# Running the ffn of a selective-scan block for two rows at a time, and summing softplus on TensorE

## The chip, the cores and the metric

One core of one Trainium2 chip. The metric is the time on the device in microseconds of one execution of the whole program; a kernel's figure is the median of several runs.

## What is computed

The input x is an image batch of 8 x 48 x 48 tokens with 256 channels, all float32. The block is:

```python
x = x + ss2d(ln(x))                      # L0_conv
t = x.reshape(8, 48 * 48, 256)
t = t + ffn(ln(t))                       # L0_ffn
```

`ss2d` projects to 512 channels twice (xh and z), runs a depthwise 3 x 3 convolution on xh, derives from it dt (rank 8, then `softplus`), B and C (16 states each), and scans over all 2304 positions:

```python
dtN = softplus(dt) @ W_dtN + b_dtN
h = exp(softplus(dt) * A) * h + (dtN * B) * x_t        # 512 channels x 16 states, 8 images
y = sum_n(h * C) + Dskip * x_t
out = (layernorm(y) * silu(z)) @ W_out + b_out
```

`ffn` is no matrix product. It reads three 16-wide one-hot fields and three flags of each normalised token (the first element over 0.5 of each field), shifts an 8-bit number by a 4-bit amount to the left or to the right, and adds 2.0 at the places of the low and of the high nibble of the result, in channels 64 to 87:

```python
hot = x > 0.5
val = first16(32) + 16 * first16(40); sa = first16(48)
res = where(act_shl, (val << sa) & 255, where(act_shr, val >> sa, 0))
out = x; out[64:80] += amp * one_hot(res & 15); out[72:88] += amp * one_hot(res >> 4)
```

Since t + ffn(ln(t)) holds t twice, once plain and once normalised, the kernel has to scale and shift each token's 256 channels once more: res * (1 + rs2) - mean * rs2.

## The kernel before

**Steps and rows.** The scan has 2304 steps, one for each position; a row of the image is 48 steps (slots 0 to 47), and four steps are a quad. The 128 partitions of the state hold 2 halves of the channels x 8 images x 8 pairs of states; each step works on 256 channels x 2 states in the free dimension. VectorE owns the first 192 of the 256 channels, GpSimd the other 64.

For each step VectorE runs four instructions: `decay_state` (L894 and L897: decay times the last state, one for each of the two states) and `add_input` (L910 and L913: x times db, plus that). The decays come from ScalarE: `decay` (L668) fills a PSUM tensor `ps_a` for two steps, with two such buffers, so ScalarE can be at most some two to three steps ahead of VectorE; `decay_pool` (L678) does the same for GpSimd, four steps at a time. GpSimd runs `pool_input` (L1161, the product of x and db for a quad), `pool_decay` (L1171) and `pool_add` (L1181). TensorE sums the states with C (`sum_states`, L510) after each quad, over a ring of 8 steps, and adds the skip term.

**Side work.** Everything else of a row, before and after its scan, is laid between the steps of other rows. The table `AT` (L40) says for each stage the step at which each of its parts is due, counted from the row's first step: `"ffn": (96, 96, 97, ...)` means that the ffn of row r runs while row r + 2 is scanned, its first two parts in slot 0. Each engine walks through all rows and slots in program order and does what is due. On VectorE `between(i, s, place)` is called twice per step: place 0 lies between `decay_state` and `add_input`, place 1 behind `add_input`; ffn parts with an even number go to place 0, those with an odd one to place 1. On ScalarE and GpSimd the side work stands behind the step's own instructions. All engines are in order, so a wait in a side part holds the decays or states behind it. Two PSUM banks (`ps_s`) are shared by all of TensorE's stages in turn.

**The softplus chain.** For row r, in slots relative to its first step: the convolution (-48 to -44) is copied to `xc`, projected (-43) and gives dt before softplus in the shared banks (-42 and -39). ScalarE's `softplus_parts` (L718 and L719) writes |dt| to `dt` and relu(dt) to `dttok`; `softplus_exp` and `softplus_log` (L725 and L730, both at -35, that is slot 13) make log(1 + exp(-|dt|)) of `dt` in place. GpSimd's `finish_dt` (L1201, at -34 and -29) adds the two. Then TensorE transposes the sum (L588, -26 to -23) and projects it to dtN (L597, -21); ScalarE's `copy_dttok` (L707) brings the tokens to `dttok`, which by then is free, and SP's queue stores them to DRAM (L377), from where they are loaded back, spread over the partitions, as `dtb` (L402). x goes the same way: `transpose_xc` (L565), `copy_xtok` (L703) to `xtok`, twelve stores for a row (L368), loads to `xb` (L393).

**The ffn.** After the output projection VectorE adds the residual (L973), takes statistics (L978, L984), ScalarE makes the reciprocal deviation (L770, L774), and VectorE runs `ffn_stage` 0 to 11, `ffn_mark`, `ffn_weigh`, `ffn_add_low` and `ffn_add_high` (L995 to L1053) on 3 blocks of 128 tokens: stage 0 has three L995 (the normalised first 64 channels), stage 1 the three scalings of the whole residual L1001, the others work on a few elements per partition, such as L1013, L1018 and L1029 with 3. Each stage waits by semaphore for the one before. SP's queue then stores the row (L436, slot 7) and loads the next residual (L431).

## Time and profile before

| | us |
|---|---|
| median of 3 runs | 3854.43 |
| lowest and highest | 3844.46, 3861.37 |
| the profiled execution | 3850.34 |
| its span | 3848.5 |
| busy in it: VectorE | 3545.4 (92%) |
| GpSimd | 3123.7 (81%) |
| TensorE matmul | 3007.7 (78%) |
| ScalarE | 2946.9 (77%) |
| mean granted TensorE clock | 0.858 |
| DMA | 790.44 MB, mean 205 GB/s |

The profile calls the engines PE (TensorE matmul), PEld (its weight loads), DVE (VectorE), ACT (ScalarE), POOL (GpSimd) and SPq (the queue that issues the DMAs). L12 is line 12 of the kernel. A group of instructions shows its count, busy time and mean; consecutive instructions of one engine overlap by some tens of nanoseconds, so that the distance from start to start says what one costs when the engine is full. The idle time of an engine is put down to what ended it. A windows line gives the stretch and its length in us, then the busy time in it (and the count of instructions) of PE, PEld, DVE, ACT and POOL, then the granted TensorE clock as a share of full speed, the busy share of the DMA engines and the GB/s that they moved.

### The profile page before, as it was taken

How to read it: one execution, taken by the hardware profiler on the slowest of the kernel's cores; microseconds unless marked ns; L12 is line 12 of the kernel's file. 1: busy time of each engine (PE TensorE's matmuls, PEld its weight loads, DVE VectorE, ACT ScalarE, POOL GpSimd, SP SyncE). 2: the span in 40 equal slices, each digit the busy share in tenths (PEclk: the TensorE clock that was granted, in tenths of full speed). 3: DMA queues.
4: the chain of work that ended last, by engine and by line, in shares of the span. 5: the costliest groups of instructions: out<-in, count | busy, mean ns of one | idle time of the engine just before them, and what ended most of it. 6: DMA issues, size and time to landing. Idle time of an engine off the chain costs nothing.

```text
span 3848.5 us, 105654 instructions
## 1 busy us (share of the span) xinstructions
PE 3007.7 (78%) x34944; PEld 1624.3 (42%) x34944; DVE 3545.4 (92%) x12174; ACT 2946.9 (77%) x6050; POOL 3123.7 (81%) x5772
## 2 busy tenths in 40 slices
PE   4787888788778887888788878877887788778765
PEld 2344444444444444444444444444444444444332
DVE  2699999999999999999999999999999999999997
ACT  2678777887787778787888787778887888787764
POOL 0688888888888888888888888888888888888885
PEclk7788888888888998888799888988888889988877
DMA  2878887887788878887888778778887888788874
GB/s 60 214 196 216 223 212 201 215 226 205 206 214 220 210 209 211 216 215 209 210 223 215 207 209 223 207 205 208 221 218 205 214 212 222 205 213 217 211 189 105
DMA packets 397438, 790.44 MB, mean 205 GB/s; under 512 B 94553, under 2 KB 249178, under 8 KB 396890
## 3 DMA queue, kind: packets, MB, share of 16 engines
q1 hardware_dynamic: 396890, 783.68, 78.4%
q8 instruction: 277, 4.54, 0.5%
q14 instruction: 271, 2.22, 0.2%
HBM read 648.20 MB, written 96.73 MB: 194 GB/s over the span
## 4 chain that ended last, share of the span: by engine, by line
DVE 43%; ACT 22%; PE 17%; issue 8%; DMA 3%; POOL 3%; SPq 2%; ACTq 0%; POOLq 0%; DVEq 0%
DVE h L910 9%; DVE ps_a L894 7%; ACT ps_a L668 7%; DVE ps_a L897 6%; DVE h L913 6%; PE ps_s L615 4%; PE ps_y L510 3%; ACT ap L678 3%; PE ps_s L577 3%; DVE sz L966 2%; DVE res L1001 2%; ACT y L753 2%; ACT yn L803 2%; PE ps_y L494 2%; ACT xtok L703 2%
## 5 line engine op out<-in xcount | busy, mean ns | idle before, releaser
L668 ACT ACTIVATE ps_a<-dtb,a_n 128x384 f32<-128x384 f32 x2304 | 1252.8, 580 | 387.5 <-DVE h L913 375.7
L1181 POOL TENSOR_TENSOR h<-mp,up 128x128 f32<-128x128 f32 x2304 | 1056.6, 459 | 392.3 <-PE ps_y L510 171.1
L1171 POOL TENSOR_TENSOR mp<-ap,h 128x128 f32<-128x128 f32 x2304 | 1053.9, 457 | 111.3 <-ACT ap L678 0.8
L894 DVE TENSOR_TENSOR ps_a<-ps_a,h 128x192 f32<-128x192 f32 x2304 | 817.4, 355 | 162.1 <-ACT ps_a L668 158.6
L910 DVE SCALAR_TENSOR_TENSOR h<-xb,db,ps_a 128x192 f32<-128x192 f32 x2304 | 923.5, 401 | 7.3 <-PE ps_y L510 4.2
L913 DVE SCALAR_TENSOR_TENSOR h<-xb,db,ps_a 128x192 f32<-128x192 f32 x2304 | 929.7, 404 | 0.0
L510 PE MATMUL ps_y<-h,cw 64*32 64x256 f32 x18432 | 771.3, 453 | 126.1 <-POOL h L1181 75.8
L897 DVE TENSOR_TENSOR ps_a<-ps_a,h 128x192 f32<-128x192 f32 x2304 | 810.0, 352 | 0.0
L678 ACT ACTIVATE ap<-dtb,a_n 128x256 f32<-128x256 f32 x1152 | 521.6, 504 | 154.1 <-POOL h L1181 127.8
L1161 POOL TENSOR_TENSOR up<-xb,db 128x512 f32<-128x512 f32 x576 | 611.5, 1062 | 0.0
L510 PEld LDWEIGHTS ps_y<-h,cw 64*32 64x32 f32 x18432 | 317.1, 120 | 490.4 <-issue 244.0
L546 PE MATMUL ps_s<-xs,conv_w 96*32 96x384 f32 x4608 | 399.3, 496 | 4.9 <-ACT xc L686 4.9
L529 PE MATMUL ps_s<-xlnT,win 128*128 128x384 f32 x768 | 277.9, 507 | 53.4 <-ACT xlnT L780 53.4
L536 PE MATMUL ps_s<-xlnT,win 128*128 128x384 f32 x768 | 289.2, 509 | 14.8 <-DVE sz L966 13.1
L565 PE MATMUL ps_s<-ident,xc 128*128 128x128 f32 x576 | 137.3, 396 | 207.9 <-ACT xtok L703 194.1
L615 PE MATMUL ps_s<-wout,yn 128*128 128x256 f32 x1152 | 288.9, 394 | 2.4 <-POOL yn L1206 2.4
L577 PE MATMUL ps_s<-xp,wdt 9*128 9x192 f32 x768 | 206.0, 675 | 104.9 <-ACT xp L695 99.5
L1201 POOL TENSOR_TENSOR dt<-dt,dttok 128x768 f32<-128x768 f32 x96 | 174.1, 1814 | 91.9 <-ACT dt L730 91.9
L615 PEld LDWEIGHTS ps_s<-wout,yn 128*128 128x128 f32 x1152 | 208.1, 190 | 80.4 <-issue 50.4
L546 PEld LDWEIGHTS ps_s<-xs,conv_w 96*32 96x32 f32 x4608 | 141.5, 111 | 237.5 <-issue 231.5
L607 PE MATMUL ps_s<-swap,y 128*128 128x128 f32 x576 | 141.2, 393 | 122.6 <-ACT y L753 101.7
L494 PE MATMUL ps_y<-skip_w,xc 128*32 128x128 f32 x4608 | 200.8, 329 | 42.4 <-ACT y L794 42.4
(112 smaller groups left out, 4103.7 us busy)
## 6 DMA issues: line engine op xcount, KB each, us to landing
xb<-xd SPq DMA_DIRECT2D x576, 512.0 KB, 7.2
dtb<-xd SPq DMA_DIRECT2D x576, 512.0 KB, 7.0
xs<-xh SPq DMA_DIRECT2D x196, 192.0 KB, 3.6
xd<-dttok SPq DMA_DIRECT2D x288, 128.0 KB, 7.0
xin<-in_x_dram SPq DMA_DIRECT2D x144, 128.0 KB, 4.3
xd<-xtok SPq DMA_DIRECT2D x192, 96.0 KB
res<-in_x_dram SPq DMA_DIRECT2D x144, 128.0 KB, 5.8
out_dram<-res SPq DMA_DIRECT2D x144, 128.0 KB, 2.4
```

Of the source, the lines that this page charges most:

```text
L510: mm = pe.matmul(ps_y[32 * j:32 * j + 32, half, 0:HALF], weights[part, q * P + 32 * j:q * P + 32 * j + 32], h[part, (4 * Q + j) % HRING, n ...
L546: mm = pe.matmul(bank[32 * c:32 * c + 32, 0:TOK], conv_w[0:96, r % 3, dx, NG * c + g, :], xs[0:96, g, c, dx * IMAGES:dx * IMAGES + TOK], s ...
L615: pe.matmul(bank[:, 0:DM], yn[:, g, k * P:(k + 1) * P], wout[:, g, :], start=g == 0, stop=False)
L668: ins = act.activation(ps_a[buf][:, n, 0:2 * VD].rearrange("p (t d) -> p t d", t=2), dtb[:, u % DUNITS, 2 * buf:2 * buf + 2, 0:VD], ACT.Ex ...
L678: ins = act.activation(ap[:, Q % 2, :, n, :], dtb[:, Q % DUNITS, :, VD:HALF], ACT.Exp, scale=a_n[:, n:n + 1])
L894: dve.tensor_tensor(a[:, 0], a[:, 0], last[:, 0], ALU.mult).then_inc(m0_done, 1)
L897: dve.tensor_tensor(a[:, 1], a[:, 1], last[:, 1], ALU.mult).then_inc(m1_done, 1)
L910: dve.scalar_tensor_tensor(h[:, G % HRING, 0, 0:VD], x_t, db[:, r % 2, 0, w:w + 1], a[:, 0], ALU.mult, ALU.add).then_inc(h0_ready, 1)
L913: dve.scalar_tensor_tensor(h[:, G % HRING, 1, 0:VD], x_t, db[:, r % 2, 1, w:w + 1], a[:, 1], ALU.mult, ALU.add).then_inc(h_ready, 1)
L1161: pool.tensor_tensor(up[:, Q % 2], x4, db4.broadcast_to([P, 4, 2, VP]), ALU.mult).then_inc(u_ready, 1)
L1171: pool.tensor_tensor(mp[:, G % 2], ap[:, Q % 2, G % 4], h[:, (G - 1) % HRING, :, VD:HALF], ALU.mult) \
L1181: pool.tensor_tensor(h[:, G % HRING, :, VD:HALF], mp[:, G % 2], up[:, Q % 2, G % 4], ALU.add) \
```

## The change

It has three parts, and a new table of slots.

1. **The ffn runs for two rows together.** All its tensors, `res` among them, hold 6 blocks of tokens instead of 3, and its parts are due after odd rows only. There are 13 stages (the six L995 take two). All stand at place 1. The scaling of the residual moves to ScalarE (`scale_res`), in place, one instruction for each block. `hots` is gone; its place is taken by part of `score`. The store of a pair is six DMAs.
2. **Softplus is summed on TensorE.** relu(dt) has a tensor of its own, `rel`, and GpSimd's `finish_dt` is gone. Each transpose of the sum becomes two that accumulate in PSUM, one of `rel` and one of `dt`, and the projection to dtN runs over both. The transposed tokens go to `xtok`, since `dttok` is gone: the copy waits for the row's x to be stored, and the next row's `copy_xtok` for dt to be stored.
3. **GpSimd's side work stands between `pool_decay` and `pool_add`**, and `pool_input` of a quad stands there in the last step of the quad before.

```diff
-    "conv": (-48, -47, -45, -44), "xproj": (-43,), "dtp": (-42, -42, -39, -39), "xtok": (-34, -33, -32),
+    "conv": (-48, -47, -46, -44), "xproj": (-43,), "dtp": (-41, -41, -39, -39), "xtok": (-38, -34, -33),
     "dttok": (-26, -24, -23), "dtn": (-21,), "yt": (66, 67, 68, 69), "out": (76, 77, 80), "z": (33, 34, 36, 37),
-    "xlnT": (-153, -152), "proj": (-150, -149, -147, -146), "exp": (-35, -35), "log": (-35, -35),
+    "xlnT": (-154, -152), "proj": (-149, -148, -146, -145), "exp": (-39, -33), "log": (-38, -31),
-    "copy_y": (22, 35, 54), "y_log": (55,), "y_scale": (55,), "y_norm": (62, 63, 64), "ln1_log": (-177,),
+    "copy_y": (22, 36, 52), "y_log": (56,), "y_scale": (58,), "y_norm": (61, 61, 63), "ln1_log": (-176,),
...
-    "y_stats": (22, 45, 53), "y_shift": (57,), "residual": (77, 78, 81), "ln2_stats": (78, 81, 82),
+    "y_stats": (26, 54, 54), "y_shift": (59,), "residual": (78, 81, 82), "ln2_stats": (79, 83, 83),
...
-    "ffn": (96, 96, 97, 97, 98, 98, 99, 99, 100, 100, 101, 101, 102, 102, 103, 103), "dt_add": (-34, -29),
-    "cw": (-6, 13, 28), "gate": (68, 69, 70, 71), "store": (103,), "stack": (-141,), "load_res": (59,),
-    "bounce": (-17,), "states": (-5,), "load_xin": (-191,),
+    "ffn": (94, 95, 96, 96, 97, 97, 97, 97, 98, 101, 102, 102, 102, 104, 104, 104, 104), "cw": (-1, 14, 19),
+    "gate": (68, 70, 71, 72), "store": (106,), "stack": (-137,), "load_res": (66,), "bounce": (-15,), "states": (-6,),
+    "load_xin": (-200,), "res_scale": (97, 99, 99, 99, 101, 102),
...
 def transpose_dt(r, k):
     if k == 0:
-        pe.wait_ge(dt_ready, r * 2 + 2)
+        pe.wait_ge(sp_log, r * 2 + 2)
     bank = take_bank("dttok", r, k)
     for g in range(NG):
-        mm = pe.transpose(bank[:, g * P:(g + 1) * P], dt[:, g, k * P:(k + 1) * P], ident[:])
+        pe.matmul(bank[:, g * P:(g + 1) * P], rel[:, g, k * P:(k + 1) * P], ident[:], start=g == 0, stop=False,
+                  is_transpose=True, skip_group_check=True)
+        mm = pe.matmul(bank[:, g * P:(g + 1) * P], dt[:, g, k * P:(k + 1) * P], ident[:], start=False,
+                       stop=g == NG - 1, is_transpose=True, skip_group_check=True)
...
 def copy_xtok(r, k):
     if r >= 1 and k == 0:
-        act.wait_ge(x_stored, r * 2 * len(X_PARTS) * SEM_DMA)
+        act.wait_ge(dt_stored, r * 2 * KT * SEM_DMA)
...
 def copy_dttok(r, k):
     act.wait_ge(dttok_done, r * KT + k + 1)
-    act.activation(dttok[:, k * DI:(k + 1) * DI], shared_bank("dttok", r, k)[:], ACT.Copy) \
+    if k == 0:
+        act.wait_ge(x_stored, (r + 1) * 2 * len(X_PARTS) * SEM_DMA)
+    act.activation(xtok[:, k, :], shared_bank("dttok", r, k)[:], ACT.Copy) \
        .then_inc(dttok_ready, 1)
...
 def softplus_parts(r, g):
     if r >= 1 and g == 0:
-        act.wait_ge(dt_stored, r * 2 * KT * SEM_DMA)
+        act.wait_ge(dttok_done, r * KT)
         act.wait_ge(dtn_done, r)
...
+def scale_res(pair, k):
+    if k == 0:
+        act.wait_ge(ffn, pair * FFN + 2)
+    act.activation(res[:, k, :], res[:, k, :], ACT.Identity, bias=sc2[:, k:k + 1], scale=sc1[:, k:k + 1]) \
+       .then_inc(res_scaled, 1)
...
-def ffn_stage(r, n):
+def ffn_stage(pair, n):
...
-    elif n == 1:
-        for k in range(KT):
-            dve.tensor_scalar(res[:, k, :], res[:, k, :], sc1[:, k:k + 1], sc2[:, k:k + 1],
-                              ALU.mult, ALU.subtract)
...
 def ffn_add_low(pair):
     dve.wait_ge(marked, pair * 3 + 2)
+    dve.wait_ge(res_scaled, pair * 2 * KT + 2 * KT)
...
 for r, j in due("ffn", i, s):
-    if j % 2 == place:
-        ffn_part(r, j)
+    if r % 2 == 1 and place == 1:
+        ffn_part(r // 2, j)
...
     if exists(i):
-        if s % 4 == 0:
-            pool_input(G // 4)
+        if G == 0:
+            pool_input(0)
         pool_decay(G)
+        if s % 4 == 3 and G + 1 < STEPS:
+            pool_input(G // 4 + 1)
+    side_work(i, s)
+    if exists(i):
         pool_add(G)
-    for r, j in due("dt_add", i, s):
-        finish_dt(r, j)
-    for r, j in due("cw", i, s):
-        weigh_c(r * KT + j)
-    for r, j in due("gate", i, s):
-        gate_y(r, j)
```

`side_work` holds the last two loops of the old order. The projection to dtN loops over `rel` and `dt` in the same way as the transposes.

## Rows read from the trace of the kernel before

**Rows 1.** Windows, all steps, then four stretches of one row; columns as told above.

```profile
118.00:3812.00 3694.00, 2933.75 (x34566) 1582.50 (x34566) 3507.76 (x12035) 2905.78 (x5967) 3114.89 (x5754) 0.86 0.81 211
2042.00:2060.36 18.36, 15.11 (x204) 7.12 (x198) 18.36 (x70) 10.68 (x25) 13.44 (x26) 0.91 0.70 164
2060.36:2073.56 13.20, 6.66 (x82) 2.95 (x78) 10.79 (x41) 12.62 (x25) 12.04 (x22) 0.71 0.76 196
2073.56:2095.46 21.90, 18.85 (x227) 12.38 (x228) 21.64 (x71) 18.83 (x39) 20.22 (x36) 0.86 0.96 256
2095.46:2118.24 22.78, 19.88 (x218) 9.99 (x221) 22.63 (x78) 19.18 (x39) 18.95 (x38) 1.00 0.87 222
```

**Rows 2.** Waits, whole span: who for whom, us in total, times, longest.

```profile
ACT ps_a L668 <- DVE h L913: 375.7, 299, 3.6
DVE ps_a L894 <- ACT ps_a L668: 158.6, 167, 14.2
```

**Rows 3.** Timeline of DVE, two plain steps; start us, us, what.

```profile
2008.38 0.35 DVE L894 TENSOR_TENSOR ps_a<-ps_a,h 128x192 f32<-128x192 f32 x1
2009.56 0.35 DVE L894 TENSOR_TENSOR ps_a<-ps_a,h 128x192 f32<-128x192 f32 x1
```

**Rows 4.** Groups of DVE, whole span: count, busy us, mean ns, idle before.

```profile
L946 DVE BATCH_NORM_STATS2 sty<-y 128x6 f32<-128x512 f32 x144 | 97.7, 678 | 4.8 <-ACT y L794 4.8
L1001 DVE TENSOR_SCALAR res<-res,sc 128x256 f32<-128x256 f32 x144 | 94.0, 705 | 0.1
...
L995 DVE TENSOR_SCALAR hot<-res,mv,rs 128x64 f32<-128x64 f32 x144 | 49.2, 395 | 0.6 <-ACT rs L774 0.6
L1029 DVE TENSOR_TENSOR resi<-dif,shr 128x3 int32<-128x3 f32 x48 | 39.5, 823 | 0.0
```

**Rows 5.** Timeline of DVE in the tail, after the last step.

```profile
3839.53 1.06 DVE L1001 TENSOR_SCALAR res<-res,sc 128x256 f32<-128x256 f32 x3
...
3843.18 0.17 DVE L1031 TENSOR_SCALAR rnib<-resi 128x3 int32<-128x3 int32 x1
3843.26 0.16 DVE L1032 TENSOR_SCALAR rnib<-resi 128x3 int32<-128x3 int32 x1
3843.45 0.26 DVE L1037 TENSOR_TENSOR hots<-rnib,idx 128x96 f32<-128x96 int32 x1
```

**Rows 6.** Groups of ACT, whole span.

```profile
L746 ACT ACTIVATE xin<-xin,nm,rs 128x256 f32<-128x256 f32 x144 | 87.3, 611 | 0.7 <-DVE nm L932 0.7
```

**Rows 7.** Timeline of ACT, slot 13 of the same row.

```profile
2065.00 1.59 ACT L725 ACTIVATE dt<-dt 128x768 f32<-128x768 f32 x2
...
2068.13 0.59 ACT L668 ACTIVATE ps_a<-dtb,a_n 128x384 f32<-128x384 f32 x1
```

**Rows 8.** Groups of POOL, whole span.

```profile
L1201 POOL TENSOR_TENSOR dt<-dt,dttok 128x768 f32<-128x768 f32 x96 | 174.1, 1814 | 91.9 <-ACT dt L730 91.9
```

**Rows 9.** Groups of PE, whole span.

```profile
L588 PE MATMUL ps_s<-ident,dt 128*128 128x128 f32 x576 | 87.1, 290 | 8.8 <-POOL dt L1201 5.4
L597 PE MATMUL ps_s<-dt,wdtn 128*64 128x192 f32 x768 | 74.3, 335 | 29.8 <-ACT dttok L707 29.8
```

**Rows 10.** Timeline of SP, ACT and DVE, slots 16 to 24 of the same row.

```profile
2072.41 8.51 SPq L368 DMA_DIRECT2D xd<-xtok  x12
...
2082.55 0.61 ACT L707 ACTIVATE dttok<-ps_s 128x512 f32<-128x512 f32 x1
2083.02 1.11 ACT L668 ACTIVATE ps_a<-dtb,a_n 128x384 f32<-128x384 f32 x2
...
2084.64 0.35 DVE L894 TENSOR_TENSOR ps_a<-ps_a,h 128x192 f32<-128x192 f32 x1
```

**Rows 11.** Windows, around the x stores; columns as in rows 1.

```profile
2072.00:2080.00 8.00, 5.77 (x49) 3.23 (x48) 6.19 (x21) 8.00 (x18) 7.19 (x13) 0.53 0.99 269
2080.00:2083.00 3.00, 2.23 (x60) 1.65 (x68) 3.00 (x9) 3.00 (x7) 2.92 (x6) 1.00 0.65 175
```

**Rows 12.** DMA issues on the page: KB each, median us to landing.

```profile
xd<-dttok SPq DMA_DIRECT2D x288, 128.0 KB, 7.0
```

205 lines of the change are left out of this document (107 added, 98 removed).

## Prediction, made before the changed kernel ran

> **What bounds the kernel now.** I first asked which engine is busy all the time. The steps run from 118 to 3812 us; in these 3694 us [rows 1] VectorE is busy for 3507.76 (95%), ScalarE for 2905.78, GpSimd for 3114.89 and TensorE for 2933.75 (79 to 84%). So a VectorE instruction that goes is worth something, unless another engine is late in the same stretch; the other three are full enough for that. The sum is made against the profiled execution: 3850.34 us, of which the span is 3848.5. The median of the three runs is 3854.43, so 4 us go on top at the end. 48 rows in 3694 us are 77.0 us a row, with some 118 us ahead and 36 us behind.
>
> Then I cut one row (2042.00 to 2118.24) into four stretches [rows 1]. Slots 0 to 7 take 18.36 us: VectorE is busy for all of it, TensorE for 15.11, ScalarE for only 10.68. Slots 8 to 15 take 13.20 us: VectorE 10.79, ScalarE 12.62. There ScalarE sets the pace, and VectorE stands still for 2.4 us. Slots 16 to 31 (21.90 us) and 32 to 47 (22.78 us) are VectorE's again, at 99%, with TensorE busy for 18.85 and 19.88 us. The waits say the same [rows 2]: ScalarE waits 375.7 us in all for VectorE's state update, VectorE 158.6 us for ScalarE's decays.
>
> **What VectorE loses.** A plain step starts 1.18 us after the one before (2008.38 to 2009.56) [rows 3]. Eight of them are 9.44 us; slots 0 to 7 took 18.36, so 8.92 us are side work. Statistics that stay have 1.18 us of it: L946 with 678 ns, less some 80 ns in which it overlaps its follower [rows 4], 0.6, and L919 and the aggregation the rest, read in the same way. The other 7.74 us are the ffn of one row. The largest pieces are the three L1001, 705 ns each in the mean [rows 4], less the overlap 1.9 us a row. They go to ScalarE. The three L995, 395 ns in the mean [rows 4], hold some 0.9 us a row and stay for every row. What is left, 7.74 - 1.9 - 0.9 = 4.9 us, is paid once for two rows, because these instructions cost by count, not by size: L1029 writes 3 elements and takes 823 ns in the mean [rows 4]. Their size doubles: 576 more elements per pair at 1.1 ns (from 0.16 us for L1032 with 3 and 0.26 for L1037 with 96 [rows 5]) are 0.65 us.
>
> Now several dependent stages share one slot with no step work between them: nine such neighbours per pair (96, three at 97, two at 102, three at 104). In the tail, L1031 to L1032 (independent) start 0.08 us apart and L1032 to L1037 (dependent, with a semaphore) 0.19 [rows 5]: 0.11 us each, 1.0 us per pair. The Trainium skill says otherwise ("VectorE: DVE Perf Modes", section "The DRAIN you can't avoid"): a semaphore between chained operations costs nothing extra. By it the sum would be some 24 us better; I take the rows.
>
> Per pair: 1.8 + 4.9 + 0.65 + 1.0 = 8.3 us, where it was 15.5. That is 3.6 us a row, 173 us in all, the most that this part gives if nothing else is late. Part of these costs is a collision: three L1001 take 1.06 us in the tail, with GpSimd silent [rows 5], but 1.9 in a row. Where the stages now meet GpSimd I can't see. The bounds for the 24 times 4.9 us are all small operations at tail prices (about half, 60 us less) and all like L1029 (60 us more).
>
> **What ScalarE gains and loses.** Six scalings per pair, like L746 at 611 ns [rows 6], of which some 90 ns overlap: 3.1 us per pair, 75 us in all. They lie in slots 1 to 6 of the ffn rows, where ScalarE had 7.7 us free [rows 1]; cost nothing. If that cover were gone, the 75 us would show. The first waits for the second ffn stage (VectorE, slot 95), with the decay of slot 98 behind it on ScalarE. But that decay waits for the end of step 95 anyway, so it comes about 1 us late where two steps are in store: nothing. The exps and logs of softplus stood together at slot 13: no decay between 2065.00 and 2068.13 [rows 7]. Now they stand at slots 9, 10, 15 and 17, so two halves of 1.6 us. I take half of the 2.4 us stall as gone, 1.2 us; bounds 0 and 2.4.
>
> **GpSimd.** L1201 goes, 174.1 us [rows 8]. That is off the path: VectorE does not wait for it, and GpSimd is at 81%. The product of a quad made ahead, and gates between decay and add, fill short pauses of the same idle engine; worth 0. cw moves from slot 42 to 47 and its states load by one slot, on GpSimd and SP alone; 0. What is late next without the addition is only the transpose on TensorE.
>
> **TensorE** sums instead: transposes and dtN products double, which by busy time adds 87.1 + 74.3 = 161 us [rows 9], 3.4 us a row, all in slots 22 to 27. The third stretch has TensorE at 18.85 of 21.90 us, at a granted clock of 0.86. 18.85 + 3.4 = 22.25 is just above the stretch. Nearest rows of an accumulating transpose are the plain ones; I price it the same, with 0 and double as ends. With the waits for GpSimd's addition gone I take 0 here, and the full case as a rival.
>
> **SP and DMA.** The dt tokens go to xtok, so copy_dttok (slot 23) now waits until x is stored. The twelve x stores occupy SP from 2072.41 for 8.51 us, until 2080.9 [rows 10]. The DMA share is 0.99 until 2080 and 0.65 from 2080 to 2083 [rows 11], so the backlog is gone, and x lands near 2083 or 2083.5; the copy ran at 2082.55 [rows 10]. Behind it on ScalarE is the decay for slot 24, started 2083.02, wanted by VectorE at 2084.64, 0.5 us after its end. The wait is 0.5 to 1 us, VectorE loses 0 to 0.5; four of the stores now go at slot 12; I take 0. copy_xtok's wait for the last row's dt stores is 30 slots old. Stores of a pair are six DMAs at slot 10, three per row as before; the residual load has two buffers and waits less.
>
> **Sum.** A row without ffn: slots 0 to 15 took 18.36 + 13.20 = 31.56. VectorE would need 18.36 - 7.74 + 10.79 = 21.4, but ScalarE has 10.68 + 12.62 = 23.3 of work and some 2.8 us of waits for TensorE's convolution and dt products, together 26.1. Saved: 5.5, not 7.7. A row with ffn: 31.56 + 0.5 - 1.2 = 30.9; saved 0.7. Mean 3.1 a row, 149 us for 48. The tail has six L995, longer stages and six stores, less three L1001 and less one ffn ahead of y's statistics: +1. The profiled execution comes to 3850.3 - 148 = 3702; as a median, **3706 us**.
>
> **Rivals.**
> - *All of it arrives.* ScalarE's waits for TensorE shrink and the stages meet GpSimd less: 3.6 + 1.2 = 4.8 us a row, 230 in all, 3624. For: the stall [rows 2]. Against: ScalarE's 23.3 us. 0.20.
> - *TensorE becomes the bound in slots 16 to 31.* 22.25 us of work plus the 3 us in which it already waits there is up to 25; VectorE then gets back between 0.3 and 2.8 less. In the middle, 1.7: the row gains 1.4, 67 in all, 3787. For: the fill of that stretch. Against: a TensorE that idles less may keep a higher clock. 0.20, of which 0.04 ends within 0.5%.
> - *Slower: the x stores hold ScalarE.* Place: copy_dttok at slot 23. Landings of the dt stores take 7.0 us in the median [rows 12]; with that, x is stored at 2080.9 + 7.0 = 2087.9, the copy waits 5.3 us and VectorE 4.8, against 3.1 won: +1.7 a row, 82 in all, 3936. It decides once x lands more than 3.1 + 0.5 us after 2082.55, or 5.2 us after its last issue. Against: the DMA share falling to 0.65. 0.07.
> - *The change does not do what it says,* the transposes replacing instead of adding: the same instructions in the same order, so the forecast's time. It moves no number.
> - *The gains and the costs cancel:* 0.01 within 0.5% besides the 0.04.
>
> **Numbers.** Forecast 0.52, others 0.20, 0.20, 0.07 and 0.01. A measurement of this kernel can tell about 0.5% (19 us) from no change. Faster by more: 0.52 + 0.20 + 0.16 = 0.88; within: 0.05; slower: 0.07. The likeliest case alone, with its 60 us bounds, spans 3645 to 3765; the range goes to 3625 and 3795, taking in most of the two neighbouring cases, which leaves about 2 in 10 out.
>
> **What would show it.** Right: rows in turns of about 71 and 77 us; no L1001 on VectorE, and some 8.3 us of ffn per pair; ScalarE's wait for VectorE's h clearly under 375.7 us; VectorE's wait for ps_a at about 110 us; GpSimd busy for some 2950 us, TensorE for some 3150. Wrong: VectorE waiting at slot 24 behind xtok's copy; a stall of VectorE in slots 22 to 31 put down to TensorE or to decays held up by it; or rows of equal length, which would mean that the rows without ffn gained nothing.

## The result and the profile after

The changed kernel takes 3809.69 us (median of 4 runs, 3807.05 to 3823.5), the one before 3854.43 (median of 3; a fourth execution took 8256 us and is left out). The ratio is 0.989, with a 95% interval of 0.985 to 0.993: **faster by 1.1%, some 45 us**, with an interval of about 25 to 56, where the prediction had 148. It lies above the range (3625 to 3795). The profiled execution is the slowest of the four: it took 3823.5 us, with a span of 3821.7 against 3848.5, and the prediction had 3702 for it.

The engine totals of the page, which answer to the table of before:

```profile
span 3821.7 us, 107647 instructions
...
PE 3184.7 (83%) x36288; PEld 1752.0 (46%) x36288; DVE 3364.9 (88%) x11454; ACT 3005.9 (79%) x6146; POOL 2952.4 (77%) x5676
```

VectorE is busy for 180.5 us less (3545.4 before), GpSimd for 171 less, TensorE for 177 more, ScalarE for 59 more. The work went where it was forecast. But VectorE was idle for 303 us of the span before and is for 457 now: of 180 us saved on it, 154 came back as waiting. The waits of the whole span (who for whom, us in total, times, longest) name what it waits for:

```profile
ACT ps_a L676 <- DVE h L933: 249.2, 281, 2.3
POOL h L1202 <- PE ps_y L513: 243.6, 135, 5.1
DVE ps_a L914 <- ACT ps_a L676: 238.7, 232, 10.5
...
ACT xc L694 <- PE ps_s L549: 119.8, 128, 2.8
...
ACT xtok L717 <- PE ps_s L594: 57.5, 46, 2.1
DVE h L930 <- PE ps_y L513: 55.4, 42, 3.8
...
DVE sz L986 <- ACT yn L830: 29.0, 52, 1.9
...
ACT ap L686 <- POOL h L1202: 7.4, 14, 1.6
```

Against [rows 2]: ScalarE waits for VectorE 249 us instead of 376, VectorE for ScalarE's decays 239 instead of 159, and two waits of VectorE are new, for TensorE's sums (55 us, 4 before) and for ScalarE's tanh (29, 1 before). One wait went: ScalarE's for GpSimd's state, 127.8 us before and 7.4 now. The chain that ended last was VectorE for 43% of the span; it is now TensorE for 48% and VectorE for 19%.

Where in a row? These are windows of two rows, the first without ffn in its first slots, the second with it, each cut into six stretches of eight slots (columns as in the rows of before). They answer to [rows 1], whose first two stretches are the first two here and whose others are cut in halves:

```profile
2100.53:2114.26 13.73, 12.21 (x156) 5.40 (x152) 11.42 (x41) 9.01 (x20) 9.47 (x19) 0.96 0.91 250
2114.26:2130.12 15.86, 10.63 (x147) 5.42 (x139) 11.16 (x41) 13.98 (x30) 10.74 (x22) 0.82 0.65 175
2130.12:2141.03 10.91, 9.12 (x113) 5.62 (x113) 9.69 (x33) 10.88 (x23) 9.91 (x19) 0.53 0.67 180
2141.03:2153.35 12.32, 12.32 (x149) 8.68 (x134) 11.19 (x36) 7.88 (x16) 11.08 (x21) 1.00 1.03 273
2153.35:2166.79 13.44, 12.68 (x130) 7.07 (x129) 12.91 (x45) 10.22 (x20) 11.56 (x24) 1.00 0.84 209
2166.79:2178.43 11.64, 10.63 (x120) 4.59 (x122) 11.64 (x42) 9.53 (x20) 10.23 (x21) 1.00 0.74 197
2178.43:2194.94 16.51, 12.64 (x176) 6.01 (x173) 16.30 (x59) 13.53 (x29) 8.05 (x16) 0.90 0.65 162
2194.94:2208.48 13.54, 8.39 (x103) 4.01 (x87) 12.60 (x44) 12.05 (x25) 10.73 (x22) 0.87 0.90 223
```

One row can mislead, so the windows of rows 6 to 41 were averaged by stretch, 18 rows of each kind; an "even" row has the first two ffn stages in slots 46 and 47, an "odd" row the rest in slots 0 to 8:

| slots | before, even / odd | after, even / odd | VectorE idle after |
|---|---|---|---|
| 0-7 | 18.87 / 18.63 | 13.73 / 15.80 | 2.31 / 0.21 |
| 8-15 | 13.09 / 13.23 | 15.46 / 13.43 | 4.34 / 0.91 |
| 16-23 | 10.92 / 10.76 | 10.95 / 11.31 | 1.23 / 1.59 |
| 24-31 | 11.37 / 11.46 | 12.09 / 11.80 | 0.96 / 0.68 |
| 32-39 | 12.71 / 12.73 | 13.50 / 13.52 | 0.55 / 0.56 |
| 40-47 | 10.19 / 10.42 | 11.86 / 9.43 | 0.01 / 0.00 |

Three things are to be seen. Slots 0 to 15 take 29.19 us in a row **without** the ffn and 29.23 with it: VectorE's work there differs by 5.6 us and the time not at all. In slots 24 to 31 of the first row TensorE is busy for all of the window (12.32 of 12.32). And slots 16 to 39, where the forecast had put nothing, are longer in both kinds of row, by 1.6 us a row. A whole row takes 77.6 us (even) and 75.3 (odd), where it took 77.2. So the rows without ffn gained nothing, which the prediction had named as a sign of being wrong (it had them at 71).

The ScalarE timeline at the start of the row without ffn shows how its time passes (start us, us, what, and in brackets the idle time before and what ended it):

```profile
2101.70 0.49 ACT L694 ACTIVATE xc<-ps_s 128x384 f32<-128x384 f32 x1 [1.21 <-PE ps_s L549]
...
2103.64 0.49 ACT L694 ACTIVATE xc<-ps_s 128x384 f32<-128x384 f32 x1 [0.47 <-PE ps_s L549]
...
2105.57 0.49 ACT L694 ACTIVATE xc<-ps_s 128x384 f32<-128x384 f32 x1 [0.65 <-PE ps_s L549]
...
2108.67 0.49 ACT L694 ACTIVATE xc<-ps_s 128x384 f32<-128x384 f32 x1 [1.12 <-PE ps_s L549]
...
2110.78 0.72 ACT L703 ACTIVATE xp<-ps_s,xp_one 128x192 f32<-128x192 f32 x1 [0.64 <-PE ps_s L560]
...
2113.75 0.49 ACT L728 ACTIVATE dt<-ps_s 128x384 f32<-128x384 f32 x1 [0.66 <-PE ps_s L580]
...
2119.15 0.49 ACT L728 ACTIVATE dt<-ps_s 128x384 f32<-128x384 f32 x1 [1.88 <-PE ps_s L580]
```

Each of these copies waits for a product of TensorE, 6.6 us in all, and the decays for VectorE stand behind those copies in the same queue. VectorE's timeline of the same time shows the other end, after TensorE and ScalarE in turn:

```profile
2107.07 0.37 DVE L914 TENSOR_TENSOR ps_a<-ps_a,h 128x192 f32<-128x192 f32 x1 [1.42 <-ACT ps_a L676]
...
2117.28 0.41 DVE L930 SCALAR_TENSOR_TENSOR h<-xb,db,ps_a 128x192 f32<-128x192 f32 x1 [2.41 <-PE ps_y L513]
...
2123.99 0.37 DVE L914 TENSOR_TENSOR ps_a<-ps_a,h 128x192 f32<-128x192 f32 x1 [1.53 <-ACT ps_a L676]
```

### The profile page after: what moved, and what is told of

It reads as the page before. It is cut to its first block, busy times and chain, and to the rows that moved or that the text cites. A ratio compares the mean times of both kernels' runs of the same rounds, so it can differ in the third digit from the quotient of the medians.

```text
span 3821.7 us, 107647 instructions
## 1 busy us (share of the span) xinstructions
PE 3184.7 (83%) x36288; PEld 1752.0 (46%) x36288; DVE 3364.9 (88%) x11454; ACT 3005.9 (79%) x6146; POOL 2952.4 (77%) x5676
## 4 chain that ended last, share of the span: by engine, by line
PE 48%; ACT 21%; DVE 19%; issue 6%; POOL 4%; SPq 1%; DMA 1%; ACTq 0%; POOLq 0%
PE ps_y L513 8%; PE ps_s L623 7%; ACT ps_a L676 6%; PE ps_s L549 6%; PE ps_s L580 5%; PE ps_s L539 5%; DVE h L930 5%; PE ps_y L497 4%; DVE ps_a L914 4%; DVE h L933 3%; PE ps_s L605 3%; DVE ps_a L917 3%; ACT y L763 2%; PE ps_s L592 2%; PE ps_s L624 2%
## 5 line engine op out<-in xcount | busy, mean ns | idle before, releaser
L686 ACT ACTIVATE ap<-dtb,a_n 128x256 f32<-128x256 f32 x1152 | 518.9, 502 | 12.6 <-POOL h L1202 7.4
L549 PE MATMUL ps_s<-xs,conv_w 96*32 96x384 f32 x4608 | 397.2, 494 | 3.9 <-ACT xh L804 3.1
L615 PE MATMUL ps_s<-swap,y 128*128 128x128 f32 x576 | 161.1, 414 | 261.6 <-ACT y L763 164.7
L532 PE MATMUL ps_s<-xlnT,win 128*128 128x384 f32 x768 | 301.5, 519 | 67.6 <-ACT xh L804 39.7
L539 PE MATMUL ps_s<-xlnT,win 128*128 128x384 f32 x768 | 276.8, 504 | 3.4 <-DVE sz L986 3.4
L615 PEld LDWEIGHTS ps_s<-swap,y 128*128 128x128 f32 x576 | 89.9, 199 | 360.6 <-ACT y L763 189.0
L532 PEld LDWEIGHTS ps_s<-xlnT,win 128*128 128x128 f32 x768 | 134.1, 193 | 208.4 <-ACT xh L804 93.8
L497 PE MATMUL ps_y<-skip_w,xc 128*32 128x128 f32 x4608 | 217.0, 348 | 9.0 <-ACT y L811 9.0
```

The costliest lines, as they stand in the source:

```text
L549: mm = pe.matmul(bank[32 * c:32 * c + 32, 0:TOK], conv_w[0:96, r % 3, dx, NG * c + g, :], xs[0:96, g, c, dx * IMAGES:dx * IMAGES + TOK], s ...
L686: ins = act.activation(ap[:, Q % 2, :, n, :], dtb[:, Q % DUNITS, :, VD:HALF], ACT.Exp, scale=a_n[:, n:n + 1])
```

## The experiments

All are medians of at least four runs, beside the kernel before on the same chip (3848.6 to 3855.9 in the five comparisons; each ratio with its 95% interval). The changed kernel was not run again beside them. Its ratio has the widest interval (0.985 to 0.993), so a difference from its 3809.69 us is clear only where the two intervals lie apart, and a difference of 10 us is not. "Stretch" lengths are averages over 18 rows of a kind, as above.

### What bounds slots 0 to 15

**No ffn at all**, in the kernel before. All ffn instructions of VectorE but one small one are left out, the scaling of the residual too.

```diff
-    "ffn": (96, 96, 97, 97, ..., 103, 103),
+    "ffn": (96, 103),
-                if n == 0: ... elif n == 11: ...
+                ins = dve.tensor_scalar(sc1[:], rs2[:], 1.0, None, ALU.add)
```

> The kernel before with the ffn left out (also the last scaling of the residual), so that VectorE has 7.7 us less in each row and ScalarE and TensorE the same as before. If VectorE were what bounds slots 0 to 15, 7.7 us a row would go, 370 us, to 3490 us. Theory C: slots 0 to 15 fall only from 31.9 to some 28 to 29 us, as in the changed kernel's rows without ffn (29.2): 3 to 4 us a row, 3690 us. This is the most that any cheaper ffn can give without touching the rest.

Measured: 3757.93 us, ratio 0.975 (0.973 to 0.978). Only **98 us** came of 370. Slots 0 to 15 take 30.3 and 29.7 us (31.9 before), with VectorE idle for 8.4 of them. Windows of slots 0 to 7 and 8 to 15 of one row:

```profile
2068.91:2084.32 15.41, 13.88 (x196) 6.39 (x196) 11.01 (x40) 9.88 (x23) 13.15 (x26) 0.94 0.75 178
2084.32:2098.78 14.46, 7.52 (x103) 3.62 (x84) 10.95 (x42) 13.09 (x27) 12.18 (x23) 0.85 0.95 262
```

So VectorE is not what bounds these slots, as theory C has it, and the gain is smaller still than theory C's 160 us: [rows 1] with VectorE busy for 18.36 of 18.36 us had a second limit some 2 us below it. With these slots no cheaper ffn can give more than about 98 us. Where VectorE stands still says what a part of that limit is. In slot 5 of nearly every row it waits 4 us for ScalarE's last copy of y, which is due in slot 6 and stands behind the copies of the convolution:

```profile
DVE sty L945 <- ACT y L793: 186.2, 47, 4.0
```

The kernel before has this wait twice only (4.8 us), and the changed kernel once (2.1 us), since its table has the copy at slot 4 and the statistics at slot 6.

**Exp and log left out** of the changed kernel (TensorE then waits for relu instead): softplus is not computed.

```diff
-                pe.wait_ge(sp_log, r * 2 + 2)
+                pe.wait_ge(sp_relu, r * NG + NG)
...
-                    for r, j in due("exp", i, s): softplus_exp(r, j)
-                    for r, j in due("log", i, s): softplus_log(r, j)
```

> The changed kernel with the exps and logs of softplus left out (dt is then relu plus absolute value), which takes 3.15 us a row from ScalarE in slots 9 to 17 and nothing from TensorE or VectorE. In the changed kernel slots 8 to 15 of a row without ffn take 15.46 us, of which ScalarE is busy for 13.98 and VectorE stands still for 4.34. Theory A (ScalarE's own work is the chain's limit there): these fall to some 12.5 to 13, rows with ffn by about 0.7, 16 to 24 by 0.5: 2 to 2.5 us a row, 3700 us. Theory B (TensorE's convolution and dt products are the limit, ScalarE only follows): less than 0.5 us a row, 3790 us or more.

Measured: 3743.51 us, ratio 0.972 (0.970 to 0.973), 66 us less than the changed kernel. Slots 8 to 15: 13.95 and 12.44 us (from 15.46 and 13.43).

**A third of the convolution left out** of the changed kernel: only two of the three columns of taps are applied.

```diff
-                for dx in range(3):
+                for dx in range(2):
...
```

> The changed kernel with the third column of the convolution's taps left out: TensorE has 2.7 us less in slots 0 to 4 of each row, ScalarE and VectorE the same work. Theory B: the copies of the convolution come sooner, slots 0 to 7 of the rows without ffn fall from 13.73 towards VectorE's own 11.4 and the next eight keep their length: 2 us in every second row and about 1 in the others, 1.5 a row, 3740 us. Theory A: what is won in slots 0 to 7 is lost again in 8 to 15, where ScalarE is full: 0.5 us a row or less, 3785 us or more.

Measured: 3750.87 us, ratio 0.974 (0.972 to 0.975), 59 us less. In rows without ffn slots 0 to 7 fall from 13.73 to 11.21 us, VectorE's own time, and the next eight don't give it back (14.88); rows with ffn stay as they were. One row's first two stretches:

```profile
2061.87:2073.03 11.16, 9.63 (x125) 4.43 (x121) 11.16 (x41) 8.86 (x20) 9.31 (x19) 0.98 1.04 236
2073.03:2089.17 16.14, 10.96 (x146) 5.45 (x136) 11.16 (x40) 13.97 (x30) 11.32 (x23) 0.80 0.98 220
```

The two theories were not rivals: taking 2.9 us a row of busy time from ScalarE, or 2.8 from TensorE (a third of the convolution's 397.2 us), gives 66 and 59 us. It is a serial chain, in turns the one and the other: convolution, copy, projection, copy, dt product, copy.

### TensorE's added work

**The relu half left out** of transposes and dtN projection in the changed kernel.

```diff
-                    pe.matmul(bank[...], rel[:, g, ...], ident[:], start=g == 0, stop=False, is_transpose=True, ...)
-                    mm = pe.matmul(bank[...], dt[:, g, ...], ident[:], start=False, stop=g == NG - 1, is_transpose=True, ...)
+                    mm = pe.transpose(bank[...], dt[:, g, ...], ident[:])
...
-                    for part in (rel, dt):
+                    for part in (dt,):
```

> The changed kernel with the relu half left out of the transposes and of the dtN projection, so that TensorE has its old amount of work, and GpSimd still adds nothing: softplus lacks its relu part. Theory T (TensorE's added 177 us are what took VectorE's saving back): VectorE's waits for TensorE (L930, 55 us) vanish, slots 24 to 40 come back to 24.2 us a row from 25.5, slots 16 to 24 to 10.8, some 1.8 us a row, so 3725 us against 3810. Theory C (slots 0 to 15 of the rows without ffn are held by the chain of convolution, projections and ScalarE's copies, at 29.2 us, whatever VectorE does): little comes back, at most 0.6 us a row, 3780 us.

Measured: 3788.98 us, ratio 0.983 (0.981 to 0.985): **21 us** back, which is theory C; the intervals of this ratio and of the changed kernel's only just lie apart. Slots 24 to 31 fall to 11.66 and 11.34 us; slots 32 to 39 stay (13.44 and 13.72), so they have another cause. VectorE's waits for TensorE, which theory T wanted gone, stay too:

```profile
DVE h L927 <- PE ps_y L513: 53.3, 47, 2.7
```

Nearly all of them are at slot 8, in the kernel after as in this one (52.1 and 51.7 us), at the end of the chain above. TensorE's added work is not their cause.

**GpSimd adds again**, in the changed kernel, at slots 12 and 18.

```diff
+            def finish_dt(r, half):
+                pool.wait_ge(sp_log, r * 2 + half + 1)
+                part = dt[:, 2 * half:2 * half + 2, :].rearrange("p g t -> p (g t)")
+                pool.tensor_tensor(part, part, rel[:, 2 * half:2 * half + 2, :].rearrange("p g t -> p (g t)"), ALU.add)...
```

> The changed kernel with GpSimd adding relu and log again (slots 12 and 18), single transposes and a single dtN projection; everything else as changed. Theory T: as without the relu half, since GpSimd has room (77% busy): 3725 to 3740 us. Theory C: 3780 us. If GpSimd's 174 us matter themselves (a third theory, G), this one is slower than the kernel without the relu half by 40 us or more, near 3810.

Measured: 3820.17 us, ratio 0.991 (0.989 to 0.992): 31 us slower than without the relu half, in the same comparison, so GpSimd's additions cost about that, nearest to theory G. They cost it in two places. ScalarE waits for GpSimd's state again, 126.1 us (16.4 without the relu half, 7.4 in the changed kernel), and VectorE's own instructions take 3397.3 us in all instead of 3356.7.

```profile
ACT ap L684 <- POOL h L1200: 126.1, 72, 3.2
```

Whether the exchange pays is not shown: against the changed kernel the difference is 10 us, inside its interval.

**The old slots of the residual, its statistics, sz and the second copy of y**, in the changed kernel.

```diff
-    "copy_y": (22, 36, 52), ... "residual": (78, 81, 82), "ln2_stats": (79, 83, 83), "sz": (35, 35, 36, 38),
+    "copy_y": (22, 35, 52), ... "residual": (77, 78, 81), "ln2_stats": (78, 81, 82), "sz": (34, 35, 36, 38),
```

> The changed kernel with the old slots for the residual (77, 78, 81), its statistics, the second copy of y (35) and sz (34, 35, 36, 38). In the changed kernel slots 32 to 39 take 13.50 us, in the one before 12.72: VectorE has 0.36 us more work and 0.4 more idle time there, at slot 36 behind ScalarE's tanh. Theory M (these slots are the cause): 0.7 us a row come back, 3775 us. Theory E (TensorE, 12.74 us busy of 13.50 and full in slots 24 to 31, comes late with the z products in any case): 3805 us or more.

Measured: 3840.82 us, ratio 0.997 (0.996 to 0.999): 31 us slower. Slots 32 to 39 come back to 12.74 us, but slots 24 to 31 take 13.52 and 13.10. Windows of slots 24 to 31 and 32 to 39 of one row:

```profile
2155.09:2168.73 13.64, 13.64 (x155) 9.80 (x140) 11.63 (x37) 7.88 (x16) 12.25 (x23) 1.00 1.01 282
2168.73:2181.46 12.73, 11.56 (x124) 5.94 (x124) 12.59 (x45) 10.15 (x20) 10.67 (x22) 1.00 0.75 183
```

So theory M has the place right: the new slots of the table are what makes slots 32 to 39 long. Without the relu half they stay at 13.44 and 13.72 us, and the kernel before with the new slots and no added product has 13.53 and 13.58 there (below). But the old slots cost more in the stretch ahead, where TensorE is busy for 13.64 of 13.64 us and VectorE, an instruction early, waits for its output projection (19.5 us in the changed kernel):

```profile
DVE res L994 <- PE ps_s L624: 59.2, 54, 12.3
```

### Each part alone, in the kernel before

**The ffn for two rows**: the change's stages, buffers and scaling on ScalarE, with the row's other slots as before.

```diff
-    "ffn": (96, 96, 97, 97, ..., 103, 103), ... "store": (103,), ... "load_res": (59,),
+    "ffn": (94, 95, 96, 96, 97, 97, 97, 97, 98, 101, 102, 102, 102, 104, 104, 104, 104), ...
+    "store": (106,), ... "load_res": (66,), ... "res_scale": (97, 99, 99, 99, 101, 102),
```

> The kernel before with the first part of the change alone: the ffn for two rows, its scaling on ScalarE; the sum on GpSimd, the tokens in their own buffer, the order on GpSimd and all other slots as before. Theory T: this part gives its saving in full where it is not taken back by TensorE, 2.7 us a row as in slots 0 to 15 less 0.9 for the two stages in slots 46 and 47: 1.8 a row, 3770 us, faster than the whole change. Theory S (the new slots matter as much as the rest): 3830 us, slower than the whole change.

Measured: 3879.63 us, ratio 1.006 (1.005 to 1.008): slower. The waits show why (ScalarE's decays for GpSimd, behind a load of dt):

```profile
ACT ap L684 <- DMA dtb<-xd: 163.3, 118, 3.6
```

**The same with the residual's load at slot 14.**

```diff
-    "load_res": (66,)
+    "load_res": (62,)
```

> The kernel before with the ffn for two rows alone, now with the residual loaded at slot 14 instead of 18. In the first such kernel (3880 us) slots 24 to 31 took 12.6 us instead of 11.4 in every row, with ScalarE waiting 163 us for the loads of dt; the residual's three loads stood on SP between the x stores. Theory Q (the queue's order costs this): 1.2 us a row come back, 3822 us. Theory D (the chip's memory traffic is what is late, wherever the loads stand): 3870 us or more.

Measured: 3829.07 us, ratio 0.994 (0.992 to 0.996): theory Q, 51 us for four slots of three DMAs. The wait for dt is 35.1 us. Part one, by itself, is worth 22 us. Its profiled execution (3823.9 us) is as long as that of the whole change (3823.5), and a pair of its rows takes 152.9 us in the mean, as there. In slots 0 to 15 a pair takes 60.1 us, 1.7 more than in the changed kernel, and in slots 16 to 47 92.7, as much less. By the medians the other parts together give 19 us more, at the edge of the noise (0.994, 0.992 to 0.996, beside 0.989, 0.985 to 0.993). In the first eight slots of the even rows VectorE waits here too for the late copy of y:

```profile
DVE sty L962 <- ACT y L807: 109.2, 47, 4.0
```

**Softplus summed on TensorE**: the change's transposes and projection; the sum is copied to the tile of x, once that is stored.

```diff
-                    mm = pe.transpose(bank[:, g * P:(g + 1) * P], dt[:, g, k * P:(k + 1) * P], ident[:])
+                    pe.matmul(bank[...], rel[...], ident[:], start=g == 0, stop=False, is_transpose=True, ...)
+                    mm = pe.matmul(bank[...], dt[...], ident[:], start=False, stop=g == NG - 1, is_transpose=True, ...)
...
+                if k == 0:
+                    act.wait_ge(x_stored, (r + 1) * 2 * len(X_PARTS) * SEM_DMA)
-                act.activation(dttok[:, k * DI:(k + 1) * DI], shared_bank("dttok", r, k)[:], ACT.Copy) \
+                act.activation(xtok[:, k, :], shared_bank("dttok", r, k)[:], ACT.Copy) \
```

> The kernel before with the second part alone: relu and log are summed by accumulating transposes, the dtN projection runs over both, GpSimd adds nothing, and the dt tokens go to xtok, whose copy waits for the stored x. All slots as before, so all twelve x stores are issued after slot 16. Theory W (the x stores hold ScalarE at slot 23, the prediction's slower case; the new slots, with a third of the stores at slot 12, are what avoided it): 1.5 to 4 us a row, 3925 to 4040 us. Theory N (x is stored in time in any table): TensorE's added work costs 0.5 us a row as in the changed kernel, GpSimd's additions give a little: 3860 to 3875 us.

Measured: 3919.37 us, ratio 1.017 (1.015 to 1.019). Nearer to theory W, but not by its mechanism alone: ScalarE waits for the stored x in every row, 42.1 us in all (8.3 of it once, in the first row, so 0.7 a row). The rest shows as VectorE's waits for TensorE in slots 24 to 31, which take 12.59 us (11.37 and 11.45 before): for the projection to dtN, which the kernel before has only once (5.8 us), and for the output projection behind it (31.7 us before).

```profile
DVE dbt L946 <- PE ps_s L600: 59.6, 48, 14.8
DVE res L978 <- PE ps_s L619: 47.5, 49, 12.9
```

In the changed kernel, with the first four x stores at slot 12, the wait for x is 11.2 us.

**GpSimd's order**: side work before the addition, the next four steps' input after it.

```diff
-                        if s % 4 == 0:
-                            pool_input(G // 4)
+                        if G == 0:
+                            pool_input(0)
...
-                        pool_add(G)
+                        if s % 4 == 3 and G + 1 < STEPS:
+                            pool_input(G // 4 + 1)
...
+                    if exists(i):
+                        pool_add(G)
```

> The kernel before with the third part alone: GpSimd's side work between its decay and its addition, and the quad's product made one step ahead. GpSimd is 81% busy and waits for TensorE and ScalarE; every theory so far gives 3851 us, within 10. If GpSimd's own pace counts where ScalarE waits for it (L678, 128 us in all), some 0.5 us a row, 3825 us.

Measured: 3975.85 us, ratio 1.032 (1.030 to 1.034): no theory had this. ScalarE's waits for GpSimd's state are 278.6 us, from 127.8:

```profile
ACT ap L678 <- POOL h L1181: 278.6, 135, 4.6
```

**The same with the first cw at slot 47.**

```diff
-    "cw": (-6, 13, 28),
+    "cw": (-1, 13, 28),
```

> The kernel before with the third part and one slot of the second: GpSimd's side work between decay and addition, and the first cw of a row at slot 47 instead of 42. The third part alone made the kernel 125 us slower (3976): slots 40 to 47 took 11.4 to 11.8 us instead of 10.3 and slots 24 to 31 12.5 instead of 11.4, and ScalarE waited 279 us for GpSimd's state. Theory H (GpSimd's wait for the states' load, 1.5 us a row, now stands ahead of the addition of its step and so holds its state, and ScalarE behind it): slots 40 to 47 come back, 1.3 us a row, 3910 us. Theory O (the order itself is slow, whatever it waits for): 3960 us or more.

Measured: 3855.66 us, ratio 1.002 (1.001 to 1.003). Theory H, and more than it asked for: 120 us. Slots 40 to 47 are 10.0 us again (11.4 and 11.8), and slots 0 to 7 are 1 us shorter. The wait:

```profile
ACT ap L678 <- POOL h L1181: 132.6, 83, 2.4
```

The wait that the order had put ahead of the addition was longer than the 1.5 us of theory H: GpSimd's first cw waits 3.0 us a row for its load in the run above, 140 us in all, and ScalarE's waits at slots 45 to 47 were 135 us there and are none here. So the 120 us are about the wait itself.

Beside the kernel before, this order is no change in time, but not for want of an effect. Slots 24 to 31 take 12.6 us instead of 11.4, with ScalarE waiting for GpSimd in slots 26 and 30, and slots 0 to 7 17.4 to 17.6 instead of 18.6 to 18.9. There VectorE is busy all the time in both, and its own small instructions got shorter, the one of [rows 4] with 823 ns first of all:

```profile
L1029 DVE TENSOR_TENSOR resi<-dif,shr 128x3 int32<-128x3 f32 x48 | 7.2, 150 | 0.0
```

Nothing but GpSimd's order and one slot of its cw differs between the two kernels.

**GpSimd's old order in the changed kernel**, the reverse of that edit.

```diff
-                        if G == 0:
-                            pool_input(0)
+                        if s % 4 == 0:
+                            pool_input(G // 4)
...
+                        pool_add(G)
...
-                    if exists(i):
-                        pool_add(G)
```

> The changed kernel with GpSimd's old order: the quad's product at its own first step, side work behind the addition. If the order is a gain in the new slots, as the saved pauses (GpSimd's waits for its own decay fell from 85.5 to 58.4 us) and the earlier state would have it, this is slower, 3825 to 3850 us. If it only costs, as in the old slots, it is faster than 3810; if GpSimd's pace counts nowhere, the same.

Measured: 3833.14 us, ratio 0.996 (0.995 to 0.998). In the new slots the order is a gain of some 23 us. It isn't a matter of ScalarE's waits for GpSimd, which are 3.2 us in this run and 7.4 with the new order. VectorE's own instructions take 3402.9 us here and 3364.9 with the new order: 38 us.

**The new slots**, with the ffn of one row at its old ones.

```diff
-    "xproj": (-43,), "dtp": (-42, -42, -39, -39), "xtok": (-34, -33, -32), ... "exp": (-35, -35), "log": (-35, -35),
+    "xproj": (-43,), "dtp": (-41, -41, -39, -39), "xtok": (-38, -34, -33), ... "exp": (-39, -33), "log": (-38, -31),
...
-    "cw": (-6, 13, 28), ... "store": (103,), "stack": (-141,), "load_res": (59,),
+    "cw": (-1, 14, 19), ... "store": (103,), "stack": (-137,), "load_res": (66,),
```

> The kernel before with the new slots alone, where they can be used: the ffn stays in one row at its old slots, with its store, and GpSimd adds at slots 12 and 18. Exp and log no longer stand together, y's last copy comes before its statistics. Theory S (the slots give most of the 20 us between the pair alone, 3829, and the whole change): 3825 to 3835 us. Theory R (they only fit the new parts): 3850 us or more.

Measured: 3965.36 us, ratio 1.030 (1.028 to 1.031). Theory R, by far: 115 us slower. ScalarE waits once in each row for dt's load, 124.9 us in all, and slots 8 to 15 take 15.4 us. Load of the stack, store of the row and x stores stand close together on SP in that combination (slots 7, 7 and 12); that they are what delays the load was not tried apart.

### Two attempts at a faster version

**y's normalisation later** (slots 16 to 18), in the changed kernel.

```diff
-    "copy_y": (22, ...), "y_norm": (61, 61, 63), "yt": (66, 67, 68, 69), "gate": (68, 70, 71, 72)
+    "copy_y": (23, ...), "y_norm": (64, 65, 66), "yt": (67, 68, 69, 70), "gate": (69, 71, 72, 73)
```

> The changed kernel with the normalisation of y on ScalarE at slots 16 to 18 instead of 13 to 15, and what follows from it (transposes at 19 to 22, first copy of y at 23, gates at 21 to 25). ScalarE has 2.1 us less in slots 8 to 15 and 0.7 more in 16 to 23. Theory A: the rows without ffn lose 1.5 to 2 us in slots 8 to 15, those with ffn 0.5, and slots 16 to 23, where ScalarE is full too (10.9 of 10.95 us), take 0.7 back: 0.4 us a row, 3790 us. If ScalarE's work counts fully wherever it stands and only moves, 3810 us.

Measured: 4070.4 us, ratio 1.057 (1.055 to 1.059). The 260 us are in slots 16 to 31: 14.5 and 14.3 us, where TensorE waits 341.4 us for y (164.7 in the changed kernel) and then comes late with everything else.

**The ffn three slots later**, with the scalings and the store.

```diff
-    "ffn": (94, 95, 96, 96, 97, ..., 104), "store": (106,), "res_scale": (97, 99, 99, 99, 101, 102),
+    "ffn": (97, 98, 99, 99, 100, ..., 107), "store": (109,), "res_scale": (100, 102, 102, 102, 104, 105),
```

> The changed kernel with all ffn parts, the scalings on ScalarE and the store three slots later: nothing of the ffn in slots 46 and 47, where VectorE is busy all the time, and the end of it in slots 8 to 11. If the ffn costs nothing where the chain is late (slots 0 to 15 take 29.2 us with and without it) and its full price where it is not, the 2.4 us of slots 40 to 47 in every second row go and about 1 us comes back: 0.7 us a row, 3775 us. If a store at slot 13 holds SP's queue ahead of the x stores, the loads of dt come late, and it is 3810 us or more.

Measured: 3807.92 us, ratio 0.989 (0.987 to 0.990): no change. In the even rows slots 40 to 47 fall from 11.86 to 9.45 us, as expected; in the odd rows slots 0 to 7 take 1.1 us more, and slots 16 to 23 take 12.22 instead of 11.31. ScalarE's waits for DMAs say what came in there:

```profile
ACT ap L686 <- DMA dtb<-xd: 53.4, 41, 2.9
...
ACT xtok L717 <- DMA xd<-xtok: 31.5, 23, 4.5
```

**The same with the store at slot 18 and the residual's load at slot 23,**

```diff
-    "store": (109,), ... "load_res": (66,),
+    "store": (114,), ... "load_res": (71,),
```

> The changed kernel with the ffn three slots later, as in the run before that changed nothing (3808 us), but with the store of the pair at slot 18, behind the x stores, and the residual's load at slot 23. There slots 40 to 47 had given 2.4 us every second row, and slots 16 to 31 had taken 1.2 back: ScalarE waited 31.5 us for the stored x and 53.4 for dt (11.2 and 5.0 in the changed kernel), since the six stores at slot 13 stood ahead of the x stores on SP. Theory Q (the queue): these waits go and 0.4 to 0.7 us a row stay won, 3775 to 3790 us. Theory B (the ffn costs its full price in slots 0 to 15 as well, since ScalarE and TensorE have to come past it): 3808 us again.

**and two slots later instead of three.**

```diff
-    "ffn": (97, 98, 99, 99, 100, ..., 107), ... "res_scale": (100, 102, 102, 102, 104, 105),
+    "ffn": (96, 97, 98, 98, 99, ..., 106), ... "res_scale": (99, 101, 101, 101, 103, 104),
```

> As the one with the store at slot 18, but the ffn only two slots later than in the changed kernel (96 to 106), so that slots 0 to 7 take all but its end. Theory Q: within 10 us of the other. If the wait of VectorE at slot 8 for TensorE's sum makes later parts cheaper, the other is the faster one.

Measured: 3815.59 us, ratio 0.991 (0.989 to 0.994), and 3832.03, ratio 0.995 (0.994 to 0.997). In the first the wait for the stored x is gone and slots 16 to 23 are 10.86 us, but slots 24 to 31 take 13.02: the loads of dt now stand behind the stores there.

```profile
ACT ap L686 <- DMA dtb<-xd: 91.2, 49, 3.8
```

Theory Q is right on the place and wrong on the gain: in both places that I tried for the six stores, another transfer came late behind them. With the ffn two slots later instead of three, the odd rows' slots 0 to 7 take 17.87 us instead of 16.95. No version tried is faster than the changed kernel by more than its noise.

## Why the prediction was wrong

**VectorE's saving: right.** 173 us forecast, 180.5 measured in busy time, and 169.3 with the first part alone. But that the two agree so well is partly luck: with GpSimd's old order the changed kernel would have saved 142.5 us, and this order the prediction had priced at 0. The six L995, now L1019, cost 408 ns each in the mean. Three groups of the ffn after (VectorE groups, whole span):

```profile
L1019 DVE TENSOR_SCALAR hot<-res,mv,rs 128x64 f32<-128x64 f32 x144 | 51.1, 408 | 0.0
L1023 DVE SCALAR_TENSOR_TENSOR score<-hot,score 128x96 f32<-128x96 f32 x72 | 29.8, 465 | 0.0
...
L1048 DVE TENSOR_TENSOR resi<-dif,shr 128x6 int32<-128x6 f32 x24 | 4.0, 166 | 0.8
```

The add that took 823 ns [rows 4] takes 166 now, and L1042 (128x6) takes 573: the slow instruction is another one of the chain. Each of the nine dependent neighbours leaves VectorE idle for 0.8 us in 24 times, 0.3 us a pair for all nine, on top of their own lengths; the forecast had 1.0 us a pair, in which the lost overlap is included.

**Slots 0 to 15: the sum nearly right, its parts wrong.** Forecast 26.1 and 30.9 us, 57.0 a pair; measured 29.2 and 29.2, 58.4 a pair (63.8 before). The step that failed is "some 2.8 us of waits for TensorE". That was read in a row where VectorE's ffn held ScalarE back and gave TensorE time to run ahead, so most of those waits were hidden (ScalarE waits 5.5 us for VectorE in the same slots before, and not at all in the even rows after). Without the ffn they are 6.2 us (ScalarE's idle time put down to TensorE in slots 0 to 10, mean of the even rows), and 23.0 of work plus 6.2 are the 29.2 measured. The work was priced, the waits that its cover hid were not. The row with ffn came out better, since its first two stages (2.4 us) stand in slots 46 and 47 and not, as I had it, in slots 0 to 7.

**Slots 16 to 47: the step that cost most.** I had priced them at 0 but for a rival. Measured per pair: +0.6 in slots 16 to 23, +1.1 in 24 to 31, +1.6 in 32 to 39, +0.7 in 40 to 47 (the two ffn stages less what left). That is 3.9 us a pair, 94 of the 121 us by which the profiled execution missed its 3702; slots 0 to 15, where a pair saved 5.4 us and not 6.1, are another 17. "With the waits for GpSimd's addition gone I take 0 here" was the wrong choice between two bounds: my own number, 18.85 + 3.4 = 22.25 us in a stretch of 21.90, had it over the edge before any wait. What the runs showed in its place:

- TensorE's relu half is worth 21 us, most of it in slots 24 to 31.
- The new slots of the residual, its statistics and sz, which I had not priced at all, cost the 0.8 us a row of slots 32 to 39: it stays without the relu half and goes with the old slots. They pay for it, since with the old ones VectorE waits 59.2 us for the output projection and the kernel is 31 us slower.
- VectorE waits at slot 24 in every row, 61.1 us in all and never before, for ScalarE's decays. ScalarE is busy for 10.9 of 10.95 us in slots 16 to 23, and I had named no limit for that stretch. VectorE's work there fell from 10.6 to 9.7 us and the time did not fall. This wait stays without the relu half (58.5 us) and is there in the kernel before with the new slots (50.1), so it belongs to the slots. At slot 26, behind the second copy to xtok, which waits for the transposes, are 33.7 us more, and 14.7 without the relu half.

**The rival "TensorE becomes the bound"** had the place and the sign, and its 3787 is nearer than the forecast. That nearness is in good part luck: it put 1.7 us a row, 82 us, on TensorE's added work, and leaving that out gives 21.

**ScalarE: right on the work.** The scalings cost 79.4 us of busy time (75 forecast), and the wait for the second stage 21.6. The stall behind exp and log, 2.4 us before, is 0.9 us in slots 8 to 15 of the odd rows, where the forecast had 1.2. In the even rows VectorE stands still for 4.3 us there.

**GpSimd and its order: priced at 0, and wrong.** The additions are worth some 31 us and the order some 23, in the new slots. "Idle engine" was the wrong reason. ScalarE, four steps ahead, waits for this engine's last result and not for its share of busy time: 127.8 us before, 7.4 after, 126.1 with the additions put back. And VectorE's own instructions take 38 and 41 us longer in all with the old order and with the additions; the traces show that and not by what mechanism.

**The slower rival** did not decide, for the reason given: four of the stores went early, and ScalarE waits 11.2 us for x in the whole run. Its sign, VectorE waiting at slot 24, came true all the same, for the other reason told above. In the old slots ScalarE does wait for x in every row, 0.7 us, and the kernel is slower.

**The change itself** is a set of parts of which, in the kernel before, one is faster alone (the ffn, 3829, with the queue put right), one makes no difference with one slot moved (the order, 3856), and two are slower (the sum, 3919; the slots, 3965). Together they come to 3810, well below the last three and 19 us below the first, which is at the edge of the noise. Why the sum and the slots cost 69 and 115 us alone and not together is open in part: the first four x stores at slot 12 are one reason, and the cost of the slots alone (ScalarE's wait for dt's load) was not taken apart.

## What to carry to other kernels

A busy share near 100% in a stretch says that an engine is a limit, not how far below the next one lies; leave its work out, once, before making it cheaper (here 98 us of 370). Where work is taken off an engine, price the others' waits as they will be without the cover: the waits in the trace of before are those that are left after it. On engines that work in program order, and on one DMA queue, a part placed ahead of something that others wait for passes its own wait on to them (here some 120 us for an engine that was busy for 81% of the time), so each part of such a change has to be looked at in the slots that it will have. And an engine off the path can still set how long the instructions of the full one take: 38 us here for an order.
